# Graph layers with two normalisations: fewer warm-up matmuls, no tile of negated means, and the store of the second-last group moved to ScalarE

## The reference

```
x  = layernorm(x + relu(gnn0(x, adj)))     # gated graph convolution; with 0/1 adjacency only the "loop" relation counts:
                                           #   h = x W^T;  vals = (h + b) * sigmoid(h Wg^T + bg);  adj^T @ vals
x  = layernorm(x + gnn1(x, adj))           # relation 1: (adj @ x) @ weight[0], plus a bias
layernorm(v) = (v - mean(v)) / sqrt(var(v) + 1e-5)      # over the 128 features of a node
```

## Time and profile before

| | us |
|---|---|
| median of 3 runs | 158.79 (158.68 to 159.75) |
| the profiled execution | 159.41 |
| its span, first to last instruction | 157.7 |
| around the span | 1.7 |

### The profile page before, as it was taken

The page is one execution under the profiler, slowest core; times in us unless marked ns, Lnnn a source line. Parts: engine busy times, 40 slices in busy tenths (PEclk is TensorE's granted clock), DMA queues, the critical chain, the costliest instruction groups (busy, mean ns, idle before and its releaser), DMA issues.

```text
span 157.7 us, 3520 instructions
## 1 busy us (share of the span) xinstructions
PE 148.8 (94%) x1040; PEld 136.7 (87%) x1040; DVE 124.1 (79%) x325; ACT 122.8 (78%) x255; POOL 125.7 (80%) x195
## 2 busy tenths in 40 slices
PE   7999999999999999999999999999999999999910
PEld 3688999999999999999999999999999999999800
DVE  1359988888988888887988888887888878989980
ACT  3357876979797997979797997979797997769850
POOL 0606698797979799797979799797979799797970
PEclk9999999999999999999999999999999999999995
DMA  4899999989797988979797989989693929211053
GB/s 126 292 405 394 370 389 404 390 265 389 198 382 230 331 303 258 354 241 398 177 392 209 356 290 286 340 237 373 192 393 130 381 92 303 86 69 69 4 201 138
DMA packets 19606, 42.73 MB, mean 271 GB/s; under 512 B 2177, under 2 KB 3073, under 8 KB 19585
## 3 DMA queue, kind: packets, MB, share of 16 engines
q1 hardware_dynamic: 14544, 25.76, 48.6%
q0 software_dynamic: 4752, 16.52, 30.3%
q10 hardware_dynamic: 288, 0.20, 0.4%
HBM read 34.08 MB, written 8.39 MB: 269 GB/s over the span
## 4 chain that ended last, share of the span: by engine, by line
POOL 65%; PE 15%; issue 13%; DVE 1%; POOLq 1%; ACT 0%; DVEq 0%
POOL rstd L339 31%; POOL x L353 26%; PE hg_ps L423 7%; POOL adj_sb L326 4%; POOL adjt_sb L333 3%; PE loop_ps L439 2%; PE msg_ps L458 2%; PE msg_ps L413 1%; PE y_ps L497 1%; PE hg_ps L407 1%; POOL rstd L363 1%; POOLq L59 1%; DVE s_sb L808 0%; ACT gate L607 0%; POOLq L234 0%
## 5 line engine op out<-in xcount | busy, mean ns | idle before, releaser
L339 POOL TENSOR_TENSOR rstd<-var,power 128x8 f32<-128x8 f32 (+1 forms) x36 | 53.8, 1496 | 18.5 <-DVE var L787 18.4
L423 PE MATMUL hg_ps<-w_all,xt_sb 128*128 128x256 f32 x256 | 65.7, 382 | 0.0
L353 POOL TENSOR_SCALAR x<-s_sb,mean_neg,rstd 128x128 f32<-128x128 f32 x120 | 52.2, 448 | 3.4
L423 PEld LDWEIGHTS hg_ps<-w_all,xt_sb 128*128 128x128 f32 x256 | 44.6, 193 | 4.1 <-issue 0.3
L626 ACT ACTIVATE out_sb<-z_sb,rstd 128x128 f32<-128x128 f32 x120 | 38.1, 390 | 0.4 <-POOL rstd L339 0.4
L800 DVE TENSOR_TENSOR vals<-hg_ps,gate 128x512 f32<-128x512 f32 x32 | 22.1, 690 | 19.3 <-ACT gate L607 19.3
L439 PEld LDWEIGHTS loop_ps<-vals,adj_sb 128*128 128x128 f32 x256 | 33.3, 191 | 1.9 <-issue 0.2
L598 ACT ACTIVATE hg_ps<-gate_b 128x1024 f32<-128x1024 f32 (+1 forms) x32 | 31.8, 998 | 3.2 <-DVE vals L800 2.6
L458 PEld LDWEIGHTS msg_ps<-adjt_sb,x 128*128 128x128 f32 x248 | 31.4, 191 | 3.1 <-issue 1.5
L439 PE MATMUL loop_ps<-vals,adj_sb 128*128 128x128 f32 x256 | 33.8, 275 | 0.1
L458 PE MATMUL msg_ps<-adjt_sb,x 128*128 128x128 f32 x248 | 33.2, 277 | 0.0
(11 more groups left out here) (64 smaller groups left out, 48.2 us busy)
## 6 DMA issues: line engine op xcount, KB each, us to landing
xt_sb<-x_t_dram SPq DMA_DIRECT2D x32, 256.0 KB, 4.9
x_sb<-x_dram SPq DMA_DIRECT2D x32, 256.0 KB, 4.2
out<-out_sb SPq DMA_DIRECT2D x31, 256.0 KB, 4.7
adj_sb<-adj_dram POOLq DMA_DIRECT2D x15, 512.0 KB, 5.2
adjt_sb<-adj_t_dram POOLq DMA_DIRECT2D x15, 512.0 KB, 6.5
adjt_sb<-adj_t_dram POOLq DMA_DIRECT2D x2, 256.0 KB, 6.7
first_edges<-adj_dram SPq DMA_DIRECT2D x1, 256.0 KB, 4.2
adj_sb<-adj_dram POOLq DMA_DIRECT2D x1, 256.0 KB, 6.3
```

Source lines behind the costliest of these rows:

```text
L339: nc.gpsimd.tensor_tensor(rstd[:, c % RSTD_RING, first:end, :].rearrange("p l b -> p (l b)"), var[:, c % 2, first:end, :].rearrange("p l b ...
L353: done = nc.gpsimd.tensor_scalar(x1[:, q % X1_RING, batch(b)], s_sb[:, q % S_RING, batch(b)], mean_neg[:, c % 2, b:b + 1], rstd[:, c % RST ...
L423: last = nc.tensor.matmul(hg_ps[:, q % 2, b, :], xt_sb[:, q % XT_RING, batch(b)], w_gate, start=False, stop=True, skip_group_check=True)
```

## The change

Four edits:

- Three warm matmuls stand in front of the first projection where there were five.
- The tile `mean_neg` and the DVE instruction that filled it are gone. POOL's and DVE's first normalisation take the mean from `stats` and subtract it. `offsets` forms -mean * rstd with one instruction of three operands. Since `stats` is read longer, `first_stats` waits for POOL's normalisation of the group that used the same slot of the ring; the wait for POOL in `variances` is gone.
- Group 30's second normalisation moves from DVE to ACT (`norm2` in four instructions, behind group 29).
- Group 30's store moves from SP's queue to ACT's, behind a wait for its own four instructions; SP's remaining stores are the halves of group 31.

```diff
-        mean_neg = sb("mean_neg", [P, 2, GB], F32)
...
+        def mean_of(c, b):
+            return stats[:, c % STATS_RING, b // 2, 3 * (b % 2) + 1:3 * (b % 2) + 2]
...
-            sp.wait_ge(out_dve, 1)
-            store(LAST - 1)
             for p in range(2):
                 span = slice(2 * p * P, 2 * (p + 1) * P)
-                sp.wait_ge(out_dve, p + 2)
+                sp.wait_ge(out_dve, p + 1)
...
                     done = nc.gpsimd.tensor_scalar(
                         x1[:, q % X1_RING, batch(b)], s_sb[:, q % S_RING, batch(b)],
-                        mean_neg[:, c % 2, b:b + 1], rstd[:, c % RSTD_RING, 0, b:b + 1], ALU.add, ALU.mult)
+                        mean_of(c, b), rstd[:, c % RSTD_RING, 0, b:b + 1], ALU.subtract, ALU.mult)
...
-            for _ in range(5):
+            for _ in range(3):
                 nc.tensor.matmul(msg_ps[:, :], warm[:, :], warm_wide, start=True, stop=True)
...
             norm2(GROUPS - 3, every)
+            norm2(GROUPS - 2, every)
+            act.wait_ge(out_done, GROUPS - 1)
+            act.dma_start(out[GROUPS - 2], out_sb[:, (GROUPS - 2) % OUT_RING, :])\
+                .then_inc(out_st[(GROUPS - 2) % OUT_RING], 16)
...
-                if first == 0:
-                    await_count(dve, x1_done, c - 2)
-                    ts(mean_neg[:, c % 2, :], both[:, 0:GB, 1], -1.0, None, ALU.mult)
...
-                tt(nmr[:, list(ON_ACT).index(q), :], mean_neg[:, c % 2, :], rstd[:, c % RSTD_RING, 0, :], ALU.mult)\
+                means = stats[:, c % STATS_RING, 0:2, :].rearrange("p c (i k) -> p (c i) k", k=3)[:, :, 1]
+                stt(nmr[:, list(ON_ACT).index(q), :], means, -1.0, rstd[:, c % RSTD_RING, 0, :], ALU.mult, ALU.mult)\
...
             def first_stats(q):
                 dve.wait_ge(s_done, q + 1)
+                await_count(dve, x1_done, q - STATS_RING + 1)
...
-            last_norm2(LAST - 1, 0, GB, root_count(GROUPS + 2, 1))
             last_norm2(LAST, 0, 2, root_count(GROUPS + 3, 1))
             last_norm2(LAST, 2, GB, root_count(GROUPS + 3, 2))
```

## The result

The changed kernel takes 188.75 us (median of 4 runs, 188.68 to 189.16) where the kernel before takes 159.27 beside it: a ratio of 1.185 [1.179, 1.192], 29.5 us slower. The forecast was 157.5, in a range from 156.7 to 158.7. The profiled execution took 188.69 with a span of 187.0.

The account below looks back on a forecast made before the run. The prediction took PE to be the bound, at 4.40 us a group. Its terms 0.3 + 0.15 + 0.69 + 0.15 made 1.3 us, from the 158.79 median to 157.5, in a range from 156.7 to 158.7.

Parts of the forecast that it names:

- the sentence on the means: POOL's first normalisation: the same 120 instructions, with a subtraction and a scalar from another tile, would cost nothing.
- the prediction's own sign, line 353 over 0.5 us: POOL's first normalisation, 0.448 us then: an instruction taking over 0.5 us would show the forecast wrong.
- The rival that described it: POOL's dearer subtraction: bound once an instruction costs 0.10 more; at 0.2 more about 12 us lost, 170; chance 0.02.
- The wait in `first_stats`: DVE's statistics wait for POOL's normalisation four groups back, done some 13 us earlier: no cost.
- Warm matmuls: Start of PE: two of five matmuls fewer let projections begin earlier, 0.3 us gained.
- The clock rival: PE's start: a gap before the projections delays the clock's rise, up to 160.5 us; chance 0.06, half beyond 1%.
- the 7 us that the prediction had named as a sign: PE's first projections: spacing staying at 0.43 past 7 us would show the forecast wrong.
- Means: DVE without line 786, where PE stands: before the first messages and at 145.33; together 0.15 us gained.
- SP's queue: End: without group 30's store on SP, the last store leaves at 153.59 instead of 154.28, 0.69 us gained.
- the first rival (an accident): SP's 1.20 us issue is a rare accident, so the tail gives nothing: gain 0.45, 158.3 us; chance 0.24.
- Landing: Last store's 2.8 us from issue to landing may shrink with fewer stores queued: 0.15 us gained.
- The sum without the subtraction: Whole kernel: start, means, SP's queue and landing together gain 1.3 us, taking POOL's subtraction as free.

Follow-up runs that it names:

- experiment 3: Changed kernel, but DVE negates the means in place in `stats` and POOL adds them from there; 158.71 us, ratio 0.996 to the kernel before.
- experiment 5: Kernel before with three warm matmuls in place of five and nothing else; 158.91 us against 158.91, ratio 1.0006.
- experiment 12: Changed kernel with one word changed: POOL adds the mean instead of subtracting it, leaving out its sign; 157.73 us against 159.29, ratio 0.989.
- experiment 7: Kernel before with three warm matmuls, group 30 on ACT, and DVE's flag copy one `second_sum` earlier; 159.48 us against 158.91, ratio 1.003.
- experiment 1: Kernel before with three warm matmuls and group 30 on ACT, negated means and addition kept; 158.86 us, ratio 0.996.
- experiment 4: Kernel before with only group 30's normalisation and store moved to ACT; 158.97 us, ratio 0.997.
- experiment 6: Experiment 1 with PE made to wait for DVE's first half of group 31 before its branch; 159.0 us against 158.91, ratio 1.000.
- experiment 11: Experiment 6 with group 31's second half normalised by ACT and all three last stores on SP; 159.19 us against 159.29, ratio 0.999.
- experiment 10: Changed kernel with POOL's two operations swapped, multiplying first and subtracting the mean second; 189.25 us, one run.

## Why the prediction was wrong

**The step that failed** is the sentence on the means: "On POOL the same 120 instructions run, with a subtraction and a scalar from another tile: nothing". The scalar from another tile is nothing (experiment 3). The subtraction adds 0.350 us an instruction (3.4 ns a column in place of 0.83), and the prediction's own sign, line 353 over 0.5 us, came.

**The rival that described it was worked out rightly and given 0.02.** It says that POOL becomes the bound once an instruction costs 0.10 us more. With 0.35 in its own formula: 4 x 0.35 = 1.40 a group, less the 0.40 of slack, is 1.0 in each of 29 groups, 29 us; measured 29.5. The chance was the mistake. "Nothing in the trace speaks for it" was true of the price, and spoke for nothing either: the trace of before holds no subtraction on POOL, so that its price was unknown, not zero. The nearest row, was taken as the price, although it is the price of another operation, and a rise by a quarter was enough to turn the sign. DVE's row would not have helped: the same edit there left its four normalisations at 378 ns, from 374.

That POOL was close to being the bound, the trace of before did say. Its slack was 0.40 of 4.40 us a group, and the chain of waits, which the prediction named and set aside, ran through it for most of the span:

```profile
POOL 65%; PE 15%; issue 13%; DVE 1%; POOLq 1%; ACT 0%; DVEq 0%
```

**The wait in `first_stats`**: nothing, as forecast; experiment 3 has it, and POOL's 0.80 us before the roots are back there.

**Warm matmuls**, 0.3: nothing, by 12 runs (experiment 5). The working had PE wait for the block; that the first load varies by 0.5 us between executions, and the clock's rise by more, it did not have. The 0.30 at the first messages of experiment 12 is one execution. The clock rival did not come as a loss in experiment 5; in the profile of experiment 7, though, the spacing stayed at 0.43 until 7.15 us, past the 7 us that the prediction had named as a sign.

**Means**, 0.15: not measured by itself. Experiment 12 gained 0.27 between the first messages and the sum's weights, where 0.08 was forecast for that second place, again one execution.

**SP's queue**, 0.69: wrong in the mechanism, twice. First, the last landing was not the only end. In the kernel before DVE closes behind SP (view of one line: engine, operation, duration in ns, start in us):

```profile
L64 SPq DRAIN  x1: 7/7/7, 157.3 to 157.3; - x1
L64 DVEq DRAIN  x1: 57/57/57, 157.5 to 157.5; - x1
```

In hundredths these are 157.34 and 157.45, and DVE's stands 3.4 us behind its branch. The prediction counted some 0.6 us of closing behind SP's last landing and left DVE's last multiplication where it was; by that, SP's store could go out and land earlier and the end would stay. Experiment 5 has such an execution: the last store lands at 155.83, SP closes at 156.08, DVE at 157.05, and the span ends at 157.3.

Second, the delay was laid to group 30's store, and by experiments 1, 3 and 4 it is tied to the fetch: the issue that is held ends 0.4 us behind it. The step held the case "even if it were stretched to 1.20 it ends at 153.5"; it was stretched to 1.55, 1.94 and 1.81. The doubt of the first rival (an accident) is answered by halves. In every profile but those where PE was held back (experiments 6 and 11) the fetch meets one of SP's last three issues, which is then 0.6 to 1.9 us long. But which one differs: in experiment 5, with the stores of the kernel before, group 30's issue took 0.33 and the next one 0.90. How late the last store leaves for it runs from 1.00 us in experiment 3 to 0.03 in experiment 12, where the last issue itself was held, after it had begun on time.

**Landing**, 0.15: the last store took 2.8 us in experiments 1 and 4, 2.9 in 12, as before. The term is 0. The Trainium skill (DMA: Bandwidth & Descriptors, "Issuing engines are not separate DMA queues") says that transfers from all queues run on the same 16 engines and that another issuing engine saves issue time alone. By that the term was 0 too, and these landings agree. ACT's store landed first, as forecast: in experiment 1 at 152.60 + 2.5 = 155.1, SP's last at 153.45 + 2.8 = 156.25.

**The sum without the subtraction**, 1.3 against 1.6 to 1.8 in experiment 12, is of the right size by terms of other sizes, which is luck. Two that were not foreseen make up for what was lost: POOL's shorter last root (0.27) and DVE's quicker closing. What the second is worth is not shown alone; in experiment 12's place, with the 3 us of the others behind a branch at 153.47, DVE would have closed near 156.7 in place of SP's 155.9.

Of the kernels that leave nothing out, experiments 3 and 1 are the fastest, 0.6 to 0.7 us under the kernel before; none here has both the cheaper addition and the short list of DVE.

## What to carry to other kernels

Ask of each edit whether the trace has the very operation on the very engine. Where it has not, work out the price at which the bound moves; when that is a small step from a neighbouring row, as here 0.10 on 0.448 us, measure that one instruction before the rest, or keep the form already priced, here an addition of a negated value that another engine writes. And when a queue is late, look for what overlaps the long entry, not at the entry: here, taking the work away only handed the delay to the next one. Before an earlier end is priced, see which engine closes last.

## What the runs showed of the hardware that was not expected

- On POOL, a two-operation instruction with a subtraction costs 0.36 us and 3.4 ns a column of 128 rows in float32, with an addition 0.34 us and 0.83 ns; first or second place is alike (798, 799 ns). The split rests on two widths, 64 and 128 columns. On DVE the two differ by 4 ns in 374 (four instructions each).
- Sixteen DMA issues on SP that overlap a 16 KB instruction fetch end 0.37 to 0.41 us behind the fetch's end (one, in experiment 10, 0.50), up to 1.9 us long where others have 0.33; moving the fetch away made them short in experiment 6. All sixteen begin 0.37 to 1.02 us after another issue of SP; 58 others that overlap such a fetch were not held, and what decides is open.
- From DVE's branch to its closing instruction it took 2.9 to 3.7 us in ten kernels, with an 8 KB fetch between, and 0.6 in the four whose DVE has some 32 instructions fewer, with none. That the number of instructions decides is an inference; nothing else was varied for it.
- POOL's root over two columns takes 1.08 us while DVE multiplies 512 columns, 0.81 beside a shorter multiplication and 0.70 in the same tail one root earlier. Why was not settled.
